# Second attention: the sixteen largest scores picked by a mark instead of by a difference of two exponentials

## The reference, cut to what matters

```python
scores = jnp.einsum('bqhd,bkhd->bhqk', q, k) / jnp.sqrt(jnp.float32(D)).astype(h.dtype)
top_s, top_i = jax.lax.top_k(scores, TOPK)          # TOPK = 16 of 154
attn = jax.nn.softmax(top_s, axis=-1)
vg = jnp.take_along_axis(v_bh[:, :, None, :, :], top_i[..., None], axis=3)
o = jnp.einsum('bhqk,bhqkd->bqhd', attn, vg).reshape(B, L, C)
```

## Time and profile before

| | us |
|---|---|
| median of 3 runs | 1722.9 (1711.07 to 1726.58) |
| the profiled execution | 1712.03 |
| its span, first to last instruction | 1710.2 |

### The profile page before, as it was taken

The page is one execution under the profiler, slowest core; times in us unless marked ns, Lnnn a source line. Parts: engine busy times, 40 slices in busy tenths (PEclk is TensorE's granted clock), DMA queues, the critical chain, the costliest instruction groups (busy, mean ns, idle before and its releaser), DMA issues.

```text
span 1710.2 us, 25890 instructions
## 1 busy us (share of the span) xinstructions
PE 1475.9 (86%) x9132; PEld 749.7 (44%) x9132; DVE 915.8 (54%) x2815; ACT 768.8 (45%) x1626; POOL 258.0 (15%) x504
## 2 busy tenths in 40 slices
PE   5999857788877787998898889998889789998998
PEld 3567534454644543353243333332323135453665
DVE  2555467766878785644445556665556225451111
ACT  2254445656666561224434445554445553334221
POOL 0020053443443532000000010000100001010110
PEclk9899967679898896999999989999999998999999
DMA  5022100000000001000010000000000000000000
GB/s 168 1 81 77 48 1 13 7 1 2 4 1 2 26 1 33 1 1 1 1 62 1 0 1 1 1 1 1 1 11 1 1 2 2 11 2 4 13 16 25
DMA packets 22096, 26.78 MB, mean 16 GB/s; under 512 B 4204, under 2 KB 19634, under 8 KB 21708
## 3 DMA queue, kind: packets, MB, share of 16 engines
q1 hardware_dynamic: 21059, 25.03, 4.6%
q10 hardware_dynamic: 909, 0.10, 0.0%
HBM read 21.58 MB, written 3.08 MB: 14 GB/s over the span
## 4 chain that ended last, share of the span: by engine, by line
PE 73%; ACT 9%; DVE 8%; issue 6%; POOL 3%; DMA 0%; ACTq 0%; SPq 0%; POOLq 0%; DVEq 0%
PE bank L857 27%; PE bank L814 9%; PE bank L895 7%; PE bank L829 6%; PE bank L793 5%; PE bank L772 3%; PE bank L919 3%; ACT pr L1081 2%; ACT exp_all L1098 2%; PE bank L751 2%; DVE part_max L1294 1%; ACT h_t L1023 1%; POOL probs L1402 1%; ACT left L1104 1%; PE bank L933 1%
## 5 line engine op out<-in xcount | busy, mean ns | idle before, releaser
L1081 ACT ACTIVATE pr<-bank 128x512 f32<-128x512 f32 x656 | 355.8, 596 | 458.6 <-PE bank L857 458.1
L1294 DVE TENSOR_REDUCE part_max<-bank 128x1 f32<-128x512 f32 x512 | 328.8, 685 | 283.6 <-PE bank L857 282.6
L857 PE MATMUL bank<-slot 32*128 32x512 f32 (+1 forms) x3072 | 430.8, 532 | 18.8 <-ACT pr L1081 14.1
L857 PEld LDWEIGHTS bank<-slot 32*128 32x128 f32 x3072 | 173.8, 188 | 243.4 <-issue 161.0
L1344 POOL TENSOR_SCALAR var_eps<-mean_var 128x4 f32<-128x4 f32 x24 | 5.5, 227 | 1103.9 <-DVE mean_var L1258 1103.7
L895 PE MATMUL bank<-pr,v 128*17 128x512 f32 x1024 | 138.6, 614 | 14.3 <-ACT pr L1081 14.3
L814 PE MATMUL bank<-h_t,w_m 128*128 128x512 f32 x256 | 133.2, 646 | 6.4 <-ACT h_t L1023 4.4
L1098 ACT ACTIVATE exp_all<-bank,neg 128x154 f32<-128x154 f32 x256 | 86.2, 395 | 57.8 <-POOL neg L1389 57.1
L1319 DVE MAX8 top<-bank 128x8 f32<-128x154 f32 x256 | 69.4, 312 | 65.7 <-PE bank L919 64.4
L919 PE MATMUL bank<-kc,slot 32*128 32x154 f32 x512 | 59.9, 357 | 45.1 <-ACT exp_all L1098 44.9
L1104 ACT ACTIVATE left<-left,neg 128x154 f32<-128x154 f32 x256 | 95.4, 434 | 0.0
(11 more groups left out here) (141 smaller groups left out, 1927.6 us busy)
## 6 DMA issues: line engine op xcount, KB each, us to landing
w_m<-in_L_xcond_w_m SPq DMA_DIRECT2D x1, 2048.0 KB, 8.6
w_m<-in_L_xcond_w_m SPq DMA_DIRECT2D x2, 1024.0 KB, 6.8
w<-in_L_xcond_w SPq DMA_DIRECT2D x2, 1024.0 KB, 6.6
w_ada<-in_L_xcond_w_ada SPq DMA_DIRECT2D x1, 1792.0 KB, 10.3
x_sb<-in_x SPq DMA_DIRECT2D x6, 256.0 KB, 6.6
res_row<-rows_dram SPq DMA_DIRECT2D x12, 128.0 KB, 3.4
out_x<-x_sb SPq DMA_DIRECT2D x6, 256.0 KB, 2.1
wa<-in_L_xcond_w_qkv SPq DMA_DIRECT2D x1, 768.0 KB, 7.3
```

The lines of the kernel that those rows point to most:

```text
L857: last = nc.tensor.matmul(g.bank(*tile)[:, into], left, right, start=True, stop=True)
L1081: nc.scalar.activation(m.pr[:, u % NPR, :], g.bank("s", gi, i)[:, :], ACT.Exp).then_inc(g.free("s", gi, i), 1)
L1294: nc.vector.tensor_reduce(m.part_max[:, slot, h * TB + i // 8, i // 4 % 2:i // 4 % 2 + 1], bank[:, :], axis=AX.X, op=ALU.max).then_inc(don ...
```

## The change

The second exponential (`c_exp_left`) and the two subtractions go. In their place a step `c_pick` on GpSimd first compares `left2` with -1e30 in place, over both heads of the half at once (128 x 308), which gives 1 where a score was replaced and 0 elsewhere; it then waits for its own semaphore `marked`, and multiplies that mark with the exponentials, in two instructions of the shapes of the old subtractions. `c_pick` waits for both `left2` and `exp_all`. In the plan, `c_pick` stands where `c_diff` stood; the scores, `c_exp_all`, and everything from the transposes to `o_norm` get other planned times. In the same count of half-steps the order becomes, ScalarE: exp_all (first) 0.5, copy (previous) 0.85, exp_all (second) 1.5. TensorE: transposes (previous) 0.55, scores (next unit) 0.9, values (previous) 1.25. On GpSimd the pairs at equal times stay as they were.

```diff
-                    plan.at(start + (v - 1.15) * step, ("c_score", gi, t, 0), ("c_score", gi, t, 1), ("c_scores", gi, t))
+                    plan.at(start + (v - 1.1) * step, ("c_score", gi, t, 0), ("c_score", gi, t, 1), ("c_scores", gi, t))
                     for hf in range(2):
                         t0 = start + v * step
                         plan.at(t0, ("c_top", gi, t, hf), ("c_neg", gi, t, hf))
-                        plan.at(t0 + 0.45 * step, ("c_exp_all", gi, t, hf))
-                        plan.at(t0 + 1.0 * step, ("c_exp_left", gi, t, hf), ("c_diff", gi, t, hf))
+                        plan.at(t0 + 0.5 * step, ("c_exp_all", gi, t, hf))
+                        plan.at(t0 + 1.0 * step, ("c_pick", gi, t, hf))
                         v += 1
                     t1 = start + v * step
-                    plan.at(t1 + 0.9 * step, ("c_tail", gi, t), ("c_turn", gi, t))
-                    plan.at(t1 + 1.3 * step, ("c_copy", gi, t))
-                    plan.at(t1 + 1.8 * step, ("c_pv", gi, t))
+                    plan.at(t1 + 0.55 * step, ("c_tail", gi, t), ("c_turn", gi, t))
+                    plan.at(t1 + 0.85 * step, ("c_copy", gi, t))
+                    plan.at(t1 + 1.25 * step, ("c_pv", gi, t))
                     if t % 4 == 3:
-                        plan.at(t1 + 2.3 * step, ("o_copy", gi, half))
-                        plan.at(t1 + 2.7 * step, ("o_turn", gi, half))
-                        plan.at(t1 + 3.2 * step, ("o_norm", gi, half))
+                        plan.at(t1 + 1.6 * step, ("o_copy", gi, half))
+                        plan.at(t1 + 2.0 * step, ("o_turn", gi, half))
+                        plan.at(t1 + 2.4 * step, ("o_norm", gi, half))
...
-        elif kind == "c_exp_left":
-            v = plan.order[step]
-            for hh in range(2):
-                act.wait_ge(m.left2_done, 2 * v + hh + 1)
-                last = nc.scalar.activation(m.left2[:, v % 4, hh, :], m.left2[:, v % 4, hh, :], ACT.Exp, bias=m.neg2[:, v % 4, hh:hh + 1])
-            last.then_inc(m.left_exp, 1)
...
-            since(pool, (m.left_exp, v - 3))
+            since(pool, (m.all_done, v - 3))
...
-        elif kind == "c_diff":
+        elif kind == "c_pick":
             _, gi, t, hf = step
             v = plan.order[step]
             u = v // 2
-            pool.wait_ge(m.left_exp, v + 1)
+            pool.wait_ge(m.left2_done, 2 * v + 2)
+            pool.wait_ge(m.all_done, v + 1)
             since(pool, (m.turned, 2 * (u - 1)))
...
-            nc.gpsimd.tensor_tensor(m.tails[:, u % 2, hh, 0:TAIL], m.exp_all[:, v % 4, :, P:S2], m.left2[:, v % 4, :, P:S2], ALU.subtract)
-            nc.gpsimd.tensor_tensor(m.probs[:, u % 2, hh, :], m.exp_all[:, v % 4, :, 0:P], m.left2[:, v % 4, :, 0:P],
-                                    ALU.subtract).then_inc(m.diff_done, 1)
+            left, weights = m.left2[:, v % 4, :, :], m.exp_all[:, v % 4, :, :]
+            nc.gpsimd.tensor_scalar(left, left, -FAR, None, ALU.is_equal).then_inc(m.marked, 1)
+            pool.wait_ge(m.marked, v + 1)
+            nc.gpsimd.tensor_tensor(m.tails[:, u % 2, hh, 0:TAIL], left[:, :, P:S2], weights[:, :, P:S2], ALU.mult)
+            nc.gpsimd.tensor_tensor(m.probs[:, u % 2, hh, :], left[:, :, 0:P], weights[:, :, 0:P], ALU.mult).then_inc(m.pick_done, 1)
```

More of the change, by code:

```diff
@@ L514, in memory @@
     m.picked, m.left1_done, m.left2_done = sem("picked"), sem("left1_done"), sem("left2_done")
[L516 to L520, removed]
+    m.silu_c_done, m.silu_done, m.o_copied, m.all_done = (
+        sem(n) for n in ("silu_c_done", "silu_done", "o_copied", "all_done"))
+    m.ident_done, m.consts, m.var_done, m.rstd_done, m.row_added, m.out_gated, m.m2_gated, m.neg_done, m.pick_done, m.mask_set, m.marked = (
+        sem(n) for n in ("ident_done", "consts", "var_done", "rstd_done", "row_added", "out_gated", "m2_gated", "neg_done", "pick_done", "mask_set", "marked"))
     return m
@@ L925, in tensor_program @@
             u = plan.n("c_copy", gi, t)
-            pe.wait_ge(m.diff_done, 2 * u + 2)
+            pe.wait_ge(m.pick_done, 2 * u + 2)
             nc.tensor.transpose(bank[:, 0:P], m.tails[:, u % 2, :, :].rearrange("p h e -> p (h e)"), m.ident[:, :]).then_inc(m.turned, 1)
@@ L1094, in scalar_program @@
                 act.wait_ge(*g.group_end(7))
-            since(act, (m.diff_done, v - 3))
+            since(act, (m.pick_done, v - 3))
             bank = g.bank("c_score", *step[1:])
@@ L1325, in vector_program @@
                 nc.vector.max(m.top[:, v % 2, hh, 8:16], m.left1[:, v % 2, hh, :]).then_inc(m.picked, 1)
-            since(dve, (m.diff_done, v - 3))
+            since(dve, (m.pick_done, v - 3))
             for hh in range(2):
```

## The result

The changed kernel takes 1725.67 us (median of 20 runs, 1723.14 to 1736.22) against 1717.36 us for the kernel before (median of 20 runs, 1709.92 to 1726.58). The ratio is 1.0056, 95% interval 1.0039 to 1.0073. The forecast was 1668, with a range of 1630 to 1705, and it named faster as likely. It was wrong in sign and in size. The forecast started from the median of three runs, 1722.9; against the 1717.36 of twenty runs the same 53 us would have been 1664.

The account below looks back on a forecast made before the run. A wait loop across engines, with no engine full, was taken to bound the 441 us stage. Savings of 34 us (low clock) and 19 us (full clock) gave -53 us from 1722.9, 1669.9, taken as 1668; range 1630 to 1705.

Parts of the forecast that it names:

- The loop: Attention stage: a cross-engine wait loop sets the pace; a unit falls from 6.73 (lower clock) or 5.63 (full) to 5.0 us.
- The 39 halves with neg ahead: Of 127 halves, those with neg before the previous diff: no gain at full clock, 0.7 of the gain at the lower.
- I take 0.47 + 0.08 = 0.55 ... Ends 0.45 and 0.92: GpSimd's added mark, 128 x 308 per half: 0.47 us plus 0.08 for its own wait, all in the loop.
- the two-input line: Upper bound for the mark from GpSimd's two-input instructions: 2.12 ns a column, 187 ns fixed, 0.84 us for 308 columns.
- the two estimates set out there: Mark's price from the Trainium skill: 0.48 us at line rate, or 0.74 us for a compare body not unrolled.
- The sum from loop to stage: Converts loop savings to stage time: 34 us in the low-clock part plus 19 in the full-clock part, together -53 us.
- and is unchanged: Side work holding the loop, taken off the gain: GpSimd's other work and SiLU with table loads, about 39 us, 9%.
- POOL 185 + 128 x 0.47 = 245, so no engine is full: GpSimd's busy time in the stage after the change, beside DVE's 323 us in a stage of about 388.
- B: Rival, chance 0.15: mark at the two-input rate, 0.92 us instead of 0.55 in 88 halves; gain only 20 us, 1703.
- D: Rival, chance 0.12: transposes and copies wait for GpSimd at their queues' heads, so side work takes the gain; 1718.
- E: Rival, chance 0.10: GpSimd becomes the bound through a slow compare, mark 1.7 us, +48, 1771; slower from 1.15 us.
- Moved scores: TensorE's scores behind the transposes start 0.5 us later; slack 1.1 us, so no cost in a plain unit.

Follow-up runs that it names:

- the one-head mark: Changed kernel with the compare on one of the two heads (128 x 154), the other head's products taking left2 itself: 1706.7 us, ratio 0.9948.
- the early mark: Changed kernel with the mark waiting only for left2, so that it runs beside exp_all: 1714.5 us, ratio 0.9989.
- the control: Two exponentials in the new order, exp_left ahead of the copy, plus one GpSimd multiplication per half that nobody waits for: 1725.3 us, ratio 1.0033.

## Why the prediction was wrong, point by point

**The loop: right in its shape.** The stage bound by waits, the order 0.55, 0.85, 1.25 taking TensorE out of the loop, and the equal halves came as told: 3.09 us at the lower clock, and 3.09 again at a granted clock of 1.00 (exp_all at 560.36 and 563.45). The order alone gives 22 us with the exponentials. The 39 halves with neg ahead, put at no gain at the full clock and 0.7 of the gain at the lower one, gained 22 us.

**"I take 0.47 + 0.08 = 0.55 ... Ends 0.45 and 0.92": the first failed step, the price of the mark.** It takes 0.99, and 1.07 with its wait, outside even the upper end. I took the two-input line as an upper bound for a one-input operation, and drew the value down by a memset and a select. The runs show 2.5 ns a column against 2.12 for two inputs. With 1.07 in place of 0.55 the prediction's own sum loses 88 x 0.52 = 46 us and leaves a gain of 7; the measured change is a loss of 8.

The Trainium skill (GPSIMD Engine Reference, Engine selection), which I set beside it, has one-input work roughly at line rate; this case contradicts that by a factor of two, an estimated 0.48 us by it and 0.99 measured. Neither of the two estimates set out there, 0.48 and 0.74 us, reaches it. The first had pulled in the same wrong direction.

**The sum from loop to stage: the second failed step.** With the price right the sum is 15 us off; but with the price near its own the one-head mark gave 9 us instead of 42, and no mark at all gives 31. The two errors are not separate amounts: the line through no mark and the full mark has 36 us for each us of mark, the prediction's sum 88. Put against the loop, the mark's removal shortens 88 halves by 1.1 us, 97 us, and the time falls by 39. The starts of exp_all show it: those 88 halves took 339 us with the mark and 291 without, and the 39 others then took 16 more. I had counted only what holds the loop "and is unchanged", 39 us or 9%, and let every microsecond of the loop through. In the trace of the changed kernel 48 of the 88 halves are no more than 0.15 us above the loop's length; with one head marked 39, with the early mark 27, without the mark 19. A shorter loop is less often what a half waits for. Two things failed in it:
- "POOL 185 + 128 x 0.47 = 245, so no engine is full". It became 308 of 441 us. GpSimd's own time counts outside the plain units: 127 us of it, off the loop, cost 30 us (the control). "Added" was priced as a link of the chain, and its share as load of the queue at nothing.
- TensorE, with its side work, is close behind once the waits are gone: with a part of it left out (40 us of busy time) the version without the mark gained 29 us, the kernel before 3 to 5.

**Rivals.** B (mark at the two-input rate) was the nearest in kind, and put at 0.15 and 1703; the mark was dearer still. D's arithmetic came nearest the time, 1718, but that was luck: it took the mark at 0.55 us and laid the loss on the place of the transposes. Its sign, over 60 us of TensorE waiting at the transposes for probs and a stage unchanged, did come (68 us, and 434 against 430), and misleads: with the scores ahead of the transposes that wait is 4 us and the kernel 17 us slower, and with the exponentials in the new order it is 42 us and the kernel 22 us faster than before. E named the mark as GpSimd's burden with a break-even of 1.15 us; the break-even measured, on the line through no mark (-31 us) and 1.07 us (+8), is about 0.85 us. Of the signs to look for, the mark's length and the unit of 6.19 us, over the 5.6 that was to show the forecast wrong, worked. ScalarE's wait for the transposes fell from 110 to 76 us, not below half.

**Moved scores: "no cost in a plain unit".** Right: they start 1.15 us after exp_all in the unit shown, and the next exp_all waits for nothing but neg.

## What to carry to other kernels

When an operation moves to another engine, price it twice: as a link of the loop, and as load of that engine's queue against the other engines' time per round. Here 1 us of GpSimd a half cost the kernel 30 us even where it fitted into waits. A shorter loop is worth less than its length times its rounds, since other waits then end last in more of them: count in a trace how many rounds sit at the loop's length. When a price has no row of its own operation and form, leave the upper end open above the neighbours, and look for the algebra that needs no operation: here a factor that the normalisation removes anyway made mark and second exp both unnecessary.

## What the hardware showed that was not expected

- GpSimd's one-input operation in f32: 600 ns (compare) and 615 ns (multiply) for 128 x 154, 987 (compare) for 128 x 308, all in place, and 999 (multiply) for 128 x 309 from one tensor into another. Two inputs: 731 for 128 x 256. ScalarE's Copy with a scale took 464 ns for 128 x 308.
- Leaving out work of TensorE that had been about 56 us at the clocks of the kernel before (estimated as half of its first MLP product's 66 us and three quarters of the second's 31) took only 12 us from its busy time in the stage (331 to 319): the granted clock of the stage fell from 0.82 to 0.74.
- One more microsecond of GpSimd in each half left VectorE's busy time in the stage at 323 us (320 without it).
